# A transformer layer with mixture of experts on one core: how tokens are ranked and scattered, and where the step sizes of attention are computed

## The reference, cut to what matters

```
xn    = (x - mean) / sqrt(var + 1e-5)
# experts: 8 of them, width 512, the best 2 of each token
probs = softmax(xn @ Wg_ffn);  top_vals, top_idx = top_k(probs, 2)
out   = sum over the two of  weight * (relu(xn @ W1[e] + b1[e]) @ W2[e] + b2[e])
# attention: 8 heads, a gated delta rule over time; its per-token numbers are
beta  = sigmoid(xn @ Wb)
g     = -exp(A_log) * softplus(xn @ Wa + dt_bias)     # step size; exp(g) is the decay of a step
```

## Time and profile before

| | us |
|---|---|
| runs of the kernel before, median of 3 | 2637.5 (2637.27 to 2646.81) |
| span of the profiled execution (no time of its own beside the span is shown) | 2632.2 |
| routing, to the first work of the experts | 236.3 |
| experts: first tiles, then the steady part | 236.3 to 257, 257 to 765.5 |
| attention, from its first matmul | 779.6 to 2632.2 |
| busy over the span: PE, DVE, ACT, POOL | 2266.7, 1903.0, 1354.1, 1137.5 |

### The profile page before, as it was taken

How to read it: one execution, slowest core, us unless ns; L and a number is a source line. 1 busy time by engine, 2 the same in 40 slices (tenths; PEclk the granted TensorE clock), 3 DMA queues, 4 the chain that set the end, 5 groups by cost and what they waited for, 6 DMA issues and landing times. The chain is left out here.

```text
span 2632.2 us, 93819 instructions
## 1 busy us (share of the span) xinstructions
PE 2266.7 (86%) x36541; PEld 1651.1 (63%) x36542; DVE 1903.0 (72%) x3913; ACT 1354.1 (51%) x3667; POOL 1137.5 (43%) x1143
## 2 busy tenths in 40 slices
PE   4652999999987889899888989989898888989987
PEld 4541999999963646556565655746556565655646
DVE  5664232323228888988889899888988989888894
ACT  0001444344326655656656566655656656566663
POOL 3774444444433426253342624436253342624333
PEclk9997999999988999999999999999999999999998
DMA  5574222222210010100101000010100101000010
GB/s 168 193 248 152 72 72 73 71 72 72 72 55 21 17 44 11 36 22 25 32 15 44 21 27 23 25 44 5 42 22 25 33 14 44 23 24 22 25 29 16
DMA packets 105644, 135.05 MB, mean 51 GB/s; under 512 B 39360, under 2 KB 78816, under 8 KB 105056
## 3 DMA queue, kind: packets, MB, share of 16 engines
q0 software_dynamic: 23552, 61.38, 7.5%
q1 hardware_dynamic: 62448, 40.55, 5.8%
q10 hardware_dynamic: 19312, 28.33, 3.0%
HBM read 76.18 MB, written 54.00 MB: 49 GB/s over the span
## 5 line engine op out<-in xcount | busy, mean ns | idle before, releaser
L1458 DVE SCALAR_TENSOR_TENSOR att_cv<-att_psA,att_cw,att_cv 128x508 f32<-128x508 f32 (+2 forms) x660 | 479.2, 737 | 7.6
L1789 POOL TENSOR_TENSOR att_Sd<-att_S,att_mst 128x1024 f32<-128x1024 f32 x128 | 242.9, 1903 | 505.1 <-DVE att_S L1572 482.0
L999 PE MATMUL att_psA<-att_xt,att_wqkv 128*128 128x512 f32 x880 | 425.3, 616 | 17.0 <-DMA att_xt<-xn_cols 12.6
L1122 PE MATMUL att_psS<-att_W,att_ktok 128*128 128x128 f32 x2048 | 258.8, 280 | 12.1 <-DVE att_S L1572 6.4
L999 PEld LDWEIGHTS att_psA<-att_xt,att_wqkv 128*128 128x128 f32 x880 | 156.7, 193 | 178.7 <-issue 159.5
L734 PE MATMUL moe_psHT<-moe_xT,moe_w1s 128*128 128x128 f32 x2176 | 267.5, 276 | 0.0
L1122 PEld LDWEIGHTS att_psS<-att_W,att_ktok 128*128 128x128 f32 x2048 | 242.5, 193 | 32.9 <-issue 17.2
L675 ACT ACTIVATE moe_hT<-moe_psHT,moe_b1T 128x128 f32<-128x128 f32 x544 | 155.1, 368 | 201.1 <-PE moe_psHT L734 201.1
L744 PE MATMUL moe_psY<-moe_w,moe_hT 128*128 x1088 | 257.2, 379 | 0.0
L734 PEld LDWEIGHTS moe_psHT<-moe_xT,moe_w1s 128*128 128x128 f32 x2176 | 256.1, 193 | 0.2
L701 DVE TENSOR_TENSOR moe_y<-moe_psY,moe_b2b 128x256 f32<-128x256 f32 x136 | 57.8, 425 | 271.1 <-PE moe_psY L744 271.1
(11 more groups left out here) (247 smaller groups left out, 4382.1 us busy)
## 6 DMA issues: line engine op xcount, KB each, us to landing
expert_out<-moe_y POOLq DMA_DIRECT2D x136, 128.0 KB, 2.0
route_x_in<-in_L_attn_x_dram SPq DMA_DIRECT2D x64, 128.0 KB
xn_rows<-route_xn ACTq DMA_DIRECT2D x16, 512.0 KB, 3.6
xn_cols<-route_xnT ACTq DMA_DIRECT2D x16, 512.0 KB, 3.8
moe_w<-in_L_ffn_W_dram ACTq DMA_DIRECT2D x2, 4096.0 KB, 24.5
att_xt<-xn_cols SPq DMA_DIRECT2D x16, 512.0 KB, 4.4
att_xr<-in_L_attn_x_dram SPq DMA_DIRECT2D x64, 128.0 KB, 2.7
out_dram<-att_xr SPq DMA_DIRECT2D x256, 32.0 KB, 1.7
```

What stands on the lines that cost most here:

```text
L999: last = MM(pair_bank(m, j)[:, h, :], wqkv[:, c, (2 * j + h) * P:(2 * j + h + 1) * P], xt[:, c, :], start=(c == 0), stop=(c == DC - 1))
L1122: last = MM(pS[:, h // 4, 2 * DV * (h % 4):2 * DV * (h % 4) + 2 * DV], ktok[:, c % 2, h, :], W[:, h, 2 * two:2 * two + 2, :], start=True, ...
L1458: last = V.scalar_tensor_tensor(out=late, in0=by_lane(pair_bank(m, j)[:, h, :])[:, :, 0:LT - d], scalar=cw[:, 2 * j + h, TAPS - 1 - d:TAPS ...
L1789: G.tensor_tensor(new, old, bc(mst[:, par, c, 4 + 2 * two:6 + 2 * two, :], 3, DV), op=ALU.mult).then_inc(s["sd_done" if two else "sd_half" ...
```

## The change

The parts, in the words of the code:

- PE ranks with two matmuls a step, one with the triangle for each tile by itself and one with ones for the tile's totals; DVE copies the totals beside `taken` and runs one scan over experts and tiles (a factor of 0 in `carry` starts each expert anew); place adds the scan's result.
- POOL's scatters are written out for all eight steps; they read the slots from `where` and the rows from a wide `token` table by themselves, without copies and without the wait for earlier scatters.
- The eight blocks of zero rows are plain stores issued by SP, at a row number read from `rest`.
- SP loads the first group's rows ahead of the small parameters, and the weights of one expert (1 MB) in each step. The first step of DVE and PE is peeled, so that choose and place of step 0 come earlier. Attention's ten weight loads are issued by ACT after the loop, where the expert weights were.
- The step sizes leave routing. In the experts, the first 26 tiles of the loop are written out (`PEEL`), DVE does two linked operations after each of them, PE the sums after tiles 20, 22 and 24, ACT the exponentials, and SP stores the 2 MB after its last index load. The reciprocals are done in halves.

```diff
@@ norm_and_route, sync
+            def load_rows(i, par):
+                g = 2 * i + par
+                sp.wait_ge(xn_made, 4 * g + 4)
+                for l in range(LANES):
+                    sp.dma_start(x_in[CT * l:CT * l + CT, par], ...).then_inc(x_loaded[par], 16)
+            def load_expert(e):
+                sp.dma_start(w1[:, bass.ds(e, 1)], w1_v[:, bass.ds(e, 1)]).then_inc(w1_loaded, 16)
+                sp.dma_start(w2[:, bass.ds(e, 1)], w2_v[:, bass.ds(e, 1)]).then_inc(w2_loaded, 16)
+            load_rows(0, 0)
             sp.dma_start(w_small[:, :, 0:E], ...).then_inc(params, 16)
...
+            load_rows(0, 1)
+            load_expert(0)
+            with sp.Fori(1, NI) as i:
+                for par in range(2):
+                    load_rows(i, par)
+                load_expert(i)
+            for tile, source, loaded in (b1r, b2b):
+                sp.dma_start(tile[...], source).then_inc(loaded, 16)
+            sp.wait_ge(rest_known, 1)
+            for e in range(E):
+                row = sp.value_load(rest[0:1, e:e + 1], min_val=0, max_val=E * (N + P) - P)
+                sp.dma_start(ids_d[bass.ds(row, P), :], blank[:, :]).then_inc(rest_stored, 16)
+            sp.wait_ge(rest_stored, 16 * E)
@@ norm_and_route, gpsimd
-            def scatter(q):
-                for par in range(2):
-                    i = 2 * q + par
-                    if not (isinstance(q, int) and q == 0):
-                        pool.wait_ge(scattered[par], 2 * TI * 16 * q)
-                    pool.wait_ge(located, i + 1)
-                    pool.tensor_copy(tok[:, par, :, 0], token[:, bass.ds(TI * i, TI)]).then_inc(idx_copied, 1)
-                    pool.tensor_copy(idx[:, par], where[:, bass.ds(TI * i, TI), :]).then_inc(idx_copied, 1)
-                    pool.wait_ge(idx_copied, 2 * i + 3)
-                    ... 16 scatters from tok, idx
-            for e in range(E):
-                pool.indirect_dma_start(ids_d[:, :], ... rest[:, e:e + 1] ..., blank[:, :], None).then_inc(rest_stored, 16)
+            for i in range(NI):
+                pool.wait_ge(located, i + 1)
+                pool.sem_inc(passed, 1)
+                for t in range(TI * i, TI * i + TI):
+                    for k in range(2):
+                        pool.indirect_dma_start(ids_d[:, :], bass.IndirectOffsetOnAxis(ap=where[:, t, k:k + 1], axis=0),
+                                                token[:, t:t + WIDE], None).then_inc(scattered[i % 2], 16)
@@ norm_and_route, vector
-                link(V.tensor_tensor(place, psR[:, 0, 0:TI * E], bc(taken[:, :], 1, TI), op=ALU.add))
-                link(V.tensor_tensor(taken[:, :], psR[:, 1, 0:E], taken[:, :], op=ALU.add))
+                link(V.tensor_copy(counted[:, :, 1:TI + 1], psR[:, 1, 0:TI * E]...))
+                link(V.tensor_tensor_scan(out=before, data0=carry, data1=counted, initial=0.0, op0=ALU.mult, op1=ALU.add))
+                V.tensor_tensor(place, psR[:, 0, 0:TI * E], before[:, :, 0:TI], op=ALU.add).then_inc(placed, 1)
+                V.tensor_copy(taken, before[:, :, TI]).then_inc(placed, 1)
...
             normalise(0, 1)
             columns(0, 0)
             scale(0, 1)
-            with dve.Fori(1, NI) as i:
+            logits(0, 0)
+            columns(0, 1)
+            normalise(1, 0)
+            logits(0, 1)
+            choose_two(0)
+            scale(1, 0)
+            place_two(0)
+            normalise(1, 1)
+            columns(1, 0)
+            scale(1, 1)
+            with dve.Fori(2, NI) as i:
@@ norm_and_route, scalar
-            for tile, source, loaded in expert_params:
-                act.dma_start(tile[...], source).then_inc(loaded, 16)
+            for tile, source in attention_sources:
+                act.dma_start(tile, source).then_inc(attention_loaded, 16)
@@ norm_and_route, tensor
-                nc.tensor.matmul(psR[:, 0, 0:TI * E], tri_lt[:, :], mk, start=True, stop=False)
-                for d in range(1, TI):
-                    nc.tensor.matmul(psR[:, 0, d * E:TI * E], ones[:, :], mk[:, 0:(TI - d) * E], ...)
-                for t in range(TI):
-                    last = nc.tensor.matmul(psR[:, 1, 0:E], ones[:, :], mk[:, t * E:(t + 1) * E], ...)
+                nc.tensor.matmul(psR[:, 1, 0:TI * E], ones[:, :], mk, start=True, stop=True)
+                nc.tensor.matmul(psR[:, 0, 0:TI * E], tri_lt[:, :], mk, start=True, stop=True).then_inc(ranked, 1)
@@ experts
+            for i in range(1, PEEL):                                  # PEEL = 14
+                for tile in ((i, 1), (i + 1, 0)):
+                    step(tile, after(*tile), before(*tile))
+                    if between:
+                        between(sum(tile) + tile[0])
+            with eng.Fori(PEEL, MT // 2 - 1) as i:
...
-            for tile, source in attention_sources:                    # sync, after the first two index loads
-                sp.dma_start(tile, source).then_inc(attention_loaded, 16)
...
+            sp.wait_ge(sums_read, 2 + LANES)                          # sync, after the last index load
+            sp.wait_ge(g_step, G_STEPS)
+            sp.dma_start(stat_d, stat[:, :, :, :]).then_inc(stat_stored, 16)
+            sp.wait_ge(stat_stored, 16)
...
+            def between(t):                                           # vector; sizes yields after each of 30 links
+                for _ in range(2):
+                    next(sizes, None)
+            def between(t):                                           # tensor; TRIANGLES, LANES_01, LANES_23 = 20, 22, 24
+                if t == TRIANGLES:
+                    pe.wait_ge(g_step, G_KNOWN)
+                    for tri, bank in ((tri_le, psG[0]), (tri_gt, psG[1])):
+                        nc.tensor.matmul(bank[:, 0:NT * H], tri[:, :], stat[:, :, 1, :], ...).then_inc(sums_ready, 1)
+                for l0, at in ((0, LANES_01), (2, LANES_23)):
+                    if t == at:
+                        for l in (l0, l0 + 1):
+                            pe.wait_ge(sums_read, l + 1)
+                            nc.tensor.matmul(psG[l % 2][:, 0:NT * H], ones[r, :], stat[r, :, 1, :], ..., tile_position=(CT * l, 0)).then_inc(sums_ready, 1)
```

249 lines of the change are left out of this document (141 added, 108 removed).

## The result

The changed kernel takes 2603.2 us (median of 4 runs, 2601.6 to 2605.1), the one before 2639.5 in the same comparison (2637.3 to 2646.8): 36.2 us less, a ratio of 0.985 with a 95% interval of 0.9824 to 0.9877. The forecast was 2598 in a range of 2585 to 2618.

A forecast was written before the change was run, and what follows sets the result against it. Routing was taken as bound by two equal chains, DVE and POOL, at 21.4 us a step, experts by PE. Terms -37.4 - 8.4 + 3.6 + 1 + 2 = -39.2 took span 2632.2 to 2593.0; plus 5.3, 2598 us, range 2585 to 2618.

The forecast's parts named there:

- The block's end is POOL's: End of routing: POOL's scatters alone set it, experts start at 198.9 against 236.3 us, -37.4; rival that they do not, 5%.
- First scatter: Start of routing: rows loaded early, a peeled first step and no copies move it from 43.0 to 33.6 us.
- Steps: Routing loop: DVE's step falls from 21.4 to 17.5 us, POOL's to 20.2, so POOL is slower by 2.7 a step.
- Landing: End of routing: the last scatter lands in 2.3 us and experts begin 1.0 later.
- Scatters and full DMA: Routing loop: expert weights bring the DMA share to 0.87, priced at 0 for the loop.
- The rival of the other sign: Routing: full DMA paces scatters at 2.4 us each; with half of them so, slower than before, +74, 2672 us; chance 4%.
- Ranks and written-out scatters as a pair: Routing loop: DVE's and POOL's chains both take 21.4 us a step, so a cut in one alone would give nothing.
- Start of the experts: First tiles: without attention's weights ahead of the indices, third tile at about 12.1 us, not 20.7; -8.4 us (5 to 10).
- Step sizes in the experts: Peeled tiles: DVE's operations fit 1.9 us of room except the half reciprocals, over by 0.3; +1 us (0 to 8).
- The sums: PE in the experts: two full matmuls and four on 32 rows at the warm clock's price, +3.6 us; at routing's price 7.3.
- Statistics stored late: End of the experts: SP's 2 MB store hides, but two last gathers run beside it; +2 us (0 to 6).
- Attention: Last block, not touched by the change: as long as before within 2 us.

The follow-up runs named there:

- run 12: Changed kernel with the eight zero rows issued as indirect scatters on POOL again, not stores by SP: 2720.3 us, ratio 0.9831 to the kernel before.
- Run 7: Kernel before with only the ranks of the change (two rank matmuls, the copy and the scan): 2753.2 us, ratio 0.9919.
- run 8: Changed kernel with only the ranks put back (16 rank matmuls, no scan): 2763.4 us, ratio 0.9949 to the kernel before.
- run 11: Changed kernel with attention's weights issued again by SP in the experts, behind the first two index loads: 2727.8 us, ratio 0.9827 to the kernel before.
- run 1: Changed kernel measured again with no edit, on chip 14: 2713.5 us, ratio 0.9797 to the kernel before.
- run 2: Changed kernel with the step sizes back in routing behind its tail and the experts' loop not peeled: 2735.6 us, ratio 0.9869 to the kernel before.
- Run 4: Changed kernel with every rank step in the peeled step's order and the statistics stored in eight pieces: 2723.0 us, ratio 0.9835 to the kernel before.
- run 9: Changed kernel with POOL's first scatter waiting for all eight steps, so all scatters run behind the loop: 2734.9 us, ratio 0.9841 to the kernel before.
- run 6: Changed kernel with PE's loop over the routing steps written out, other engines as they are: 2726.4 us, ratio 0.9821 to the kernel before.

## Why the prediction held, step by step

*The block's end is POOL's.* Right: shown by run 12 on a chip with the hold, and on the first chip by the trace, where nothing but scatters runs after 163.2. The end is a sum of first scatter, 127 intervals and the way to the experts; against the forecast these gave -3.6, +5.5 and +1.5, in all +3.4 (202.3 for 198.9). Three sizes were off, and they cancelled in part.

*First scatter, forecast 33.6, was 30.0.* Rows loaded first gave 3.5 us and not 2 (the first transposes start at 11.63, before at 15.10): ACT's root waited 0.28 us for the parameters, where I had set 0.9 of the gain aside for it, and the rows came 0.8 sooner than I had put them. The other 2.1 us lie in the new order. Run 7 shows the ranks' share in it (4.0 for my 4.6 - 0.6), so it is the work taken from ahead of the first ranks that I priced too low.

*Steps.* DVE's step was forecast at 17.5 and was 17.2 (mean of the third to the seventh). The missed term is in the second step: the second located is 24.3 us behind the first (28.85 and 53.16), 7.1 more than a step. 5 of them are the order: the peeled step leaves a normalise, a column copy and a scale (29.06 to 34.1) for after its ranks, and the second step has them on top of its own. 1.9 are the wait for rows at 41.83, which stand behind the expert weights in SP's queue; I had priced the weights in the loop at nothing. POOL's sixteen scatters last 20.2, so it waits 3.9 us. I had let "POOL is slower than DVE" hold from the first step on. Stalls at the scatters added 2.6 us where I took 1, three of them, of 0.6, 0.5 and 1.5 us.

*Landing.* 4.8 us from the last scatter's start to the experts, forecast 3.3. I added 2.3 and 1.0 from the earlier trace rows, but the 2.3 may run from the end of the instruction (0.96) and not its start; with it the sum is 4.3.

*Scatters and full DMA.* The rival of the other sign did not come: 1.265 us apart at a share of 0.89, less than 3 us of stalls. This is from one trace; on the other chips the share never came so high. The rival also rested on a wrong reading of the earlier trace rows. The five intervals are not 2.4 us each but 1.6, 1.3, 2.7, 5.2 and 1.3. One of them holds a step's end, and one this pause ahead of the 114th scatter of the kernel before:

```profile
198.50 0.97 POOL L242 DMA_INDIRECT slot_tokens<-route_tok,route_idx  x1 [4.08 <-issue]
```

A pause of about 2 us stands there in every kernel, with DMA full or nearly empty. The longest of the three stalls, the 1.5 us, is this pause, and no full ring is needed for it.

*Ranks and written-out scatters as a pair.* The argument that the two chains were equal, so that both had to be cut, rests on the traces of the first chip. On the other chips the chains are not equal, and there runs 7 and 8 show the ranks' cut counting in full and the other almost not. The pair could not be parted on the first chip.

*Start of the experts.* -9.6 for -8.4, confirmed by run 11 (9.5). By its own terms the forecast should have written -8.6 (12.1 for 20.7). The second pair of indices reached POOL 1 us sooner than I had put it. On top, the product of the third tile with W1 takes 1.98 us (granted clock 1.00, 213 to 218 us) and not 3.05 (0.72, 257 to 262 us, behind the gap of 6.69 us in the earlier trace rows): the 1.1 us of the table's fourth line, which I did not have. That the shorter gap made it is not shown: in run 1 the same product took 3.47 us behind a gap of 0.83.

*Step sizes in the experts.* The peeled tiles keep 3.73 to 3.74 us but for the one behind the half reciprocal, 4.29, and small delays behind it and the sums; so the links of DVE cost 0.6 us (forecast 1, bound 8), by the mechanism that the forecast named. The sums cost 1.72 for the two full ones and 1.2 for each pair on parted rows, 4.1 in all for 3.6: the price at the higher level of the clock was the right choice, 592 ns for each matmul of 512 columns. In run 2 the same sums in routing took 2.08 us for two with a granted clock of 1.00 in the record; by duration PE is at the lower of its two levels there, 1.2 GHz. The Trainium skill, "TensorE: Matmul & The Clock Gate", The HAM clock gate, says that the array stands at 1.2 GHz after idling and that records of the gate can be unreliable; the durations of run 2 agree (PE had been idle for 36.7 us), its granted clock does not.

*Statistics stored late.* 3.0 us for 2: a wait of 2.6 and some delay behind it. Run 4 shows that it goes with the single store.

*Attention.* Forecast 0, was +7.2 between the two profiles. With the same attention code it lasted 1878.0 in the kernel before on chip 1 and between 1865.0 and 1888.7 in the changed ones, so it varies by more than that from run to run. On those chips PE's speed goes with it, roughly: PE was busy 1647.8 us in the shortest attention (run 12) and 1661.7 in the longest (run 8), and the granted clock of the whole kernel was 0.979 and 0.972. On the first chip PE was busy 1644.3 us before and 1642.3 after, so the 7.2 us are not that; their cause is open. The sum gave a span of 2593.0, and it was 2602.4: +3.4 in routing, -1.2 and -1.1 at the experts' start, +1.0 in the experts, +7.2 in attention. The 5.3 us that I added for the way from span to median were wrong too: the changed kernel's times are 1.7 us above their spans, and the rest was the profiled run of before being a fast one. That the final 2598 stands closer to 2603.2 than its sum does is luck.

## What to carry to other kernels

When two engines' chains are equally long, price each cut twice: alone it should give nothing and with the other its full size (argued here, not run on a chip with equal chains), and on another chip one of them may already be the longer, as runs 7 and 8 show. Once one engine sets a block, its end is first start, count and pace, and each instruction moved off that engine is worth its own time: count them, and look for the step at which the other engine is still late. Work that is moved into a block where PE never stops has a price there, 7.6 us here, and may have been free where it was, beside the scatters: move it last, and only if it no longer fits. A bulk load in the queue ahead of small ones is paid at the consumer's first tiles, here 9.5 us; issued from another queue in a stretch that only one engine needs, it cost at most the 1.1 us of two short stalls.

## What the runs showed of the hardware

- On three chips PE issued its small matmuls one per 0.7 to 1.4 us, with idle put down to nothing but "issue", while POOL issued indirect scatters in a row: a step became 17.5 us longer (34.7 for 17.2, changed kernel) or 18.5 (39.9 for 21.4, the one before), and PE's idle time of this kind was 96 us in the trace of run 1. With the scatters out of the loop it was gone (run 9); with PE's loop written out it stayed (run 6). The chip of the first comparison showed none of it in either kernel. Routing is longer there by 94 us in the changed kernel (296.6 for 202.3) and by 120 in the one before (356.2 for 236.3 at the experts' start). Cause open.
- POOL stood idle for 1.8 to 4.1 us between the 113th and the 114th scatter in every trace, even with the DMAs nearly empty (1.82 us at a share of 0.10, run 9). Cause open.
- DMA at a share of 0.89 and 296 GB/s for 130 us left POOL's scatters at their pace.
- Attention, untouched, lasted from 1852.6 to 1888.7 us over these profiles.
